# Up weight loads of the first attention wait for the landing of a minus-maxima row

## The reference

```python
xn = _layernorm(x, axis=-1)
x = x + _L0_attn_ref(xn, w_qkv, w_o) + _L0_ffn_ref(xn, gate_w, ..., down_sv)
xn = _layernorm(x, axis=-1)
x = x + _L1_attn_ref(xn, bv_q, bv_k, bv_v) + _L1_ffn_ref(xn, w1, w3, w2, ...)

def _L0_attn_ref(x, w_qkv, w_o):          # 32 heads of 16, 8 key/value heads, rope
    ...
    scores = jnp.einsum('bhsd,bhtd->bhst', xq, keys) * scale
    scores = jnp.where(causal, scores, -jnp.inf)
    probs = jax.nn.softmax(scores, axis=-1)
    out = jnp.einsum('bhst,bhtd->bhsd', probs, values)
    ...

def _L0_ffn_ref(x, gate_w, gate_su, gate_sv, up_w, up_su, up_sv, down_w, ...):
    a = _anemll_linear(x, gate_w, gate_su, gate_sv)   # w_eff = w * (su @ sv)
    b = _anemll_linear(x, up_w, up_su, up_sv)
    d = jax.nn.silu(a) * b
    return _anemll_linear(d, down_w, down_su, down_sv)
```

## Time and profile before

| | us |
|---|---|
| median of 3 runs | 719.05 |
| lowest and highest run | 716.56, 719.7 |
| the profiled execution | 718.95 |
| its span on the core | 717.2 |
| TensorE busy in the span | 687.6 (96%) |
| DVE, ScalarE, GpSimd busy | 415.0, 293.1, 237.6 |
| mean granted TensorE clock | 0.976 |

### The profile page before, as it was taken

How to read it: one execution, slowest core, us unless ns; L and a number is a source line. 1 busy time by engine, 2 the same in 40 slices (tenths; PEclk the granted TensorE clock), 3 DMA queues, 4 the chain that set the end, 5 groups by cost and what they waited for, 6 DMA issues and landing times. The chain is left out here.

```text
span 717.2 us, 10113 instructions
## 1 busy us (share of the span) xinstructions
PE 687.6 (96%) x3606; PEld 519.9 (72%) x3606; DVE 415.0 (58%) x982; ACT 293.1 (41%) x548; POOL 237.6 (33%) x241
## 2 busy tenths in 40 slices
PE   8997999999999999999999999879999999978998
PEld 7876666666666666666787788757888888856886
DVE  6634876776676676664377650297554554635611
ACT  4213255554555455455344232254334444332421
POOL 4465022332222222222234535233232322203443
PEclk9999799999999999999999999969999999997999
DMA  9328515323313232311155500020000100103211
GB/s 304 106 91 234 127 31 134 75 73 73 72 44 73 74 80 70 83 45 45 48 179 164 192 16 1 22 87 30 31 30 30 60 30 1 42 7 97 60 58 59
DMA packets 23147, 55.19 MB, mean 77 GB/s; under 512 B 3733, under 2 KB 4089, under 8 KB 22041
## 3 DMA queue, kind: packets, MB, share of 16 engines
q1 hardware_dynamic: 22840, 54.41, 26.5%
q10 hardware_dynamic: 256, 0.13, 0.1%
HBM read 42.86 MB, written 11.54 MB: 76 GB/s over the span
## 5 line engine op out<-in xcount | busy, mean ns | idle before, releaser
L956 DVE CUSTOM_DVE_ANT_0 bank<-bank,mask 128x512 f32<-128x512 f32 (+3 forms) x256 | 118.4, 523 | 64.1 <-PE bank L1010 63.9
L214 POOL TENSOR_TENSOR up_w_lo<-up_w_eff,up_w_hi 128x512 fp32r<-128x512 f32 x50 | 66.3, 1335 | 121.7 <-ACT up_w_hi L210 121.7
L52 PE MATMUL bank<-x0T_hi,up_w_hi 128*128 128x512 f32 x224 | 97.1, 434 | 4.8 <-DVE up_gated L280 2.5
L364 POOL TENSOR_TENSOR down_h_lo<-hidden,down_h_hi 128x512 fp32r<-128x512 f32 x50 | 65.8, 1316 | 106.6 <-ACT down_h_hi L359 106.5
L910 ACT ACTIVATE probs<-bank 128x512 f32<-128x512 f32 x160 | 85.3, 598 | 28.2 <-PE bank L1032 25.4
L54 PE MATMUL bank<-x0T_lo,up_w_hi 128*128 128x512 f32 x224 | 89.9, 401 | 0.0
L53 PE MATMUL bank<-x0T_hi,up_w_lo 128*128 128x512 f32 x224 | 89.5, 399 | 0.0
L52 PE MATMUL bank<-down_w_hi,down_h_hi 128*128 128x512 f32 x200 | 79.5, 398 | 1.1 <-DVE down_w_lo L349 0.7
L875 POOL TENSOR_SCALAR_AFFINE_SELECT probs<-probs 128x512 f32<-128x512 f32 x64 | 40.0, 637 | 122.1 <-ACT probs L910 122.1
L53 PE MATMUL bank<-down_w_hi,down_h_lo 128*128 128x512 f32 x200 | 78.9, 395 | 0.0
L54 PE MATMUL bank<-down_w_lo,down_h_hi 128*128 128x512 f32 x200 | 78.9, 394 | 0.0
(11 more groups left out here) (146 smaller groups left out, 1275.2 us busy)
## 6 DMA issues: line engine op xcount, KB each, us to landing
w_raw<-in_w_gate_up SPq DMA_DIRECT2D x25, 512.0 KB, 4.2
w_raw<-in_w_down SPq DMA_DIRECT2D x25, 256.0 KB, 2.7
q_stack<-q_hi SPq DMA_DIRECT2D x32, 128.0 KB, 3.5
att<-att_T SPq DMA_DIRECT2D x16, 256.0 KB, 2.1
q_hi<-rope_hi SPq DMA_DIRECT2D x8, 256.0 KB
q_lo<-rope_lo SPq DMA_DIRECT2D x8, 256.0 KB
q_stack<-q_lo SPq DMA_DIRECT2D x16, 128.0 KB, 3.7
attention_or_xn<-att SPq DMA_DIRECT2D x16, 128.0 KB
```

Of the source, the lines that this page charges most:

```text
L52: pe.matmul(out, w_hi, m_hi, start=first, stop=False, skip_group_check=True)
L214: pool.tensor_tensor(self.half(self.w_lo[:, o % 2], k), self.half(self.w_eff, k), f32(self.half(self.w_hi[:, o % 2], k)), ALU.subtract).th ...
L364: pool.tensor_tensor(self.h_lo[:, k % 2, :], self.hid[:, o, b * S:(b + 1) * S], f32(self.h_hi[:, k % 2, :]), ALU.subtract).then_inc(self.h ...
L956: dve.tensor_tensor_reduce(out=own, in0=own, in1=e.mask[:, S - w:S], scale=1.0, scalar=NEG, op0=ALU.add, op1=ALU.max, accum_out=rmax[:, i, ...
```

## The change

SyncE gets a wait ahead of each up load. `row_near(step)` looks from two steps back to three steps ahead for a burst in which a minus-maxima row is sent, and returns the semaphore of that row and the value that it has once the row has landed. SyncE waits for it and only then sends the load. By the schedule this gives: up(3), up(6), up(9), up(12) wait for the low row of group 0, 4, 8, 12 (sent one step earlier in the order of steps); up(5), up(8), up(11) for the high row of group 3, 7, 11 (also one step earlier), and up(4), up(7), up(10), up(13) for the high row of group 2, 6, 10, 14 (sent two steps later). up(2) finds none and is not held. The order of the transfers on SyncE's queue stays as it was.

```diff
+        def row_near(step):
+
+            for near in range(step - 2, step + EVERY + 1):
+                s = stages_of(burst_after(near)) if burst_after(near) is not None else {}
+                if s.get("high") is not None:
+                    return neg_row[1], 16 * (s["high"] + 1)
+                if s.get("low") is not None:
+                    return neg_row[0], 16 * (s["low"] + 1)
+
         def sync(sp):
             def store(g):
                 sp.wait_ge(att_out, g + 1)
@@ -848,6 +857,8 @@
                 if factor_before(step - 1) and factor_before(step - 1)[1] == 1:
                     o = factor_before(step - 1)[0] + 1
                     if o < CH0:
+                        if row_near(step):
+                            sp.wait_ge(*row_near(step))
                         up.sp_load(sp, o)
                     if o == 4:
                         sp.wait_ge(e.lr0_lo, 2 + len(LR0_REST))
```

## The result

| | before | after |
|---|---|---|
| median, 19 runs each, us | 716.75 | 714.12 |
| lowest to highest run | 714.28 to 721.11 | 712.85 to 718.19 |
| the profiled execution | 718.95 | 717.56 |
| its span | 717.2 | 715.8 |
| low row of group 0 to low row of group 15, in the profile | 243.74 | 241.25 |

The ratio after to before is 0.9965, with an interval of 0.9949 to 0.9982: 0.35% less time, about 2.5 us of the 716.75. The loop in the profile is shorter by 243.74 - 241.25 = 2.49 us, the same amount.

A forecast was written before the change was run, and what follows sets the result against it. TensorE was taken to bound the first attention, so only its waits could be regained. 2.69 us saved less 0.3 lost gave 2.39 off 718.95: 716.6 us, or 0.33% less, with an 8-in-10 range of 714.9 to 719.6.

The forecast's parts named there:

- the base of 718.95 us: Time of the profiled execution before the change, from which the forecast saving was subtracted; 0.1 below the median of 719.05.
- the same 2.39: Net saving forecast for the whole kernel in us: 2.69 saved on row waits, 0.3 lost to the factors.
- rival 1: All five waits at groups 4, 5, 8, 9, 12 go and the factors cost nothing: 715.6, or 715.5; chance 0.2.
- TensorE as the bound, the loss passing through one for one: First attention, 84 to 345 us: TensorE busy 259.09 of 261 us; each wait lengthens the loop by its idle time.
- 2.69 us booked on the loads at 5, 8 and 12: Low-row waits of 0.89, 0.68 and 1.12 us, blamed on up loads issued 0.32 us ahead of the row.
- Waits at 4 and 9 booked on the stack: Low-row waits of 0.40 and 0.23 us, 0.63 together, blamed on stack transfers and taken as no gain.
- The factors at 0.3 us, bounds 0 and 1.12: 864 KB of down-weight factors, issued later behind up(4), may make the low row of group 2 wait; cost taken 0.3.
- The prediction's last line: Signs of being wrong: groups 5, 8 and 12 still wait, or groups 2, 3, 6, 7, 10 or 11 begin to.
- A row's landing at 2.1 us or a little more: High row's time from issue to landing, 2.1 to 2.4 us expected, taken from the 256 KB store's 2.1 us.
- Rival 2: The loads are not the cause, or stack transfers take their place; only the 0.3 moves, about 719; chance 0.15.
- Rival 3: Loads behind high rows run into the following stack, delaying six low rows by at most 1.12 us each; 723.0; chance 0.08.
- the rule of the Trainium skill that spoke against the change: DMA engines alternate between queues packet by packet, so a row waits for a packet, not a load; saving near zero.

The follow-up runs named there:

- low rows only: Changed kernel with only up(3), up(6), up(9) and up(12) waiting, for the low rows of groups 0, 4, 8, 12; ratio to before 0.9958.
- changed again: The changed kernel unaltered, measured and profiled a second time against the kernel before; ratio 0.9969, loop 240.23 us.

## Why the prediction was right or wrong

**The time of 716.6 and its range were wrong, the difference was right.** The change was forecast at 0.33% less and measured at 0.35%. The median of 714.12 lies below the range's low end of 714.9. The step that failed is the first term of the sum, the base of 718.95 us from which everything was subtracted. I noted that it was 0.1 from the median of three runs and gave the base itself hardly any width; over 19 runs the median of before is 716.75, 2.2 us lower. From that base the same 2.39 gives 714.4. The low end of 714.9 left only 0.6 us below rival 1's lowest figure, 715.5, for all spread of the base, and the lowest of the three runs, 716.56, already spoke for a lower one: less 2.39 it is 714.2. The base also moves from one set of runs to another: beside the experiments its median was 718.0 in 29 runs and 716.25 in 14. The profiles show parts of the spread: the low row of group 0 is sent at 90.4 to 93.6 us in the twelve profiles, and what lies behind the last low row takes 379.8 to 381.3. The kernel before went from 243.74 to 242.74 for its loop from one profile to the next, because the waits at 3, 4 and 9 were in the first only. So the profiled execution held about 1 us of waits that come and go.

Another part lies ahead of the loop. From 75 to 80 us the granted TensorE clock was 0.50, the lower level of 1.2 GHz, in the first profile of before, and 1.00, the upper level of 2.4 GHz, in its repetition. The clock fell at 70 to 75 us (0.62) in the first and at 65 to 70 (0.66) in the repetition; TensorE had been busy for 2.7 of 5 us from 60 to 65 in both. In the four profiles with 0.50 from 75 to 80 (before, low rows only, changed, changed again) the low row of group 0 is sent at 92.0 to 93.6 us; in the six with 1.00 and without the wait for the high row of group 0, at 90.4 to 91.3. Before and changed kernels are among both, so this is spread and not an effect of the change. Over the changed kernel's 19 runs, the five with a mean granted clock of 0.976 or less took 715.2 to 718.2 us and the seven with 0.983 or more 712.9 to 713.7; in the 29 and 14 runs of before the two go together only weakly. The profiled execution of before had 0.976. What moves the drop was not tried.

**TensorE as the bound, the loss passing through one for one: right.** With waits gone at 5, 8 and 12, the spacings fell by 0.92, 0.68 and 1.13, to within 0.03 of the excess read before.

**2.69 us booked on the loads at 5, 8 and 12: right.** These waits stay wherever these loads do not move, go as each load moves, and shrink with half the bytes.

**Waits at 4 and 9 booked on the stack: partly right.** The 0.31 at group 9 without any load shows that the stack can do it alone; with load and row issued together the key score of group 9, again without a load, began 0.24 us late. At group 4 the row landed in 2.58 to 3.28 us with the stack alone, in the five kernels that show it, below the 3.64 of before; where the load stood there 0.8 to 1.05 us behind the row, no wait is listed three times (the key scores began 0.03 to 0.20 us late), and 0.43 and 0.23 once each. I called that load innocent; the runs neither clear it nor convict it. In all four cases of a wait at 4 or 9 (0.43, 0.25, 0.23, 0.31) that group's stack had a slow issue, but such issues also stand in profiles without a wait there, so that they decide is likely and not shown.

**The factors at 0.3 us, bounds 0 and 1.12: place and bounds right, the reason not.** The new wait stood at group 2, 0.92 us in one of the three profiles with the factors at that place and absent in the other two, where the stack had a slow issue. With the factors moved it left that group in two kernels whose stack came as usual. The mean of the three is 0.3 by luck: it was chosen because the factors would be nearly done, and they landed about 2.4 us after the row was sent. The prediction's last line also counts a wait that begins at group 2 as a sign of being wrong, a few lines behind allowing one there; the experiments put it down to the factors and not to the load behind a high row.

**A row's landing at 2.1 us or a little more: 1.71 in fact**, when nothing is near. up(4) then landed in 3.6 us, and in the changed kernel's profile no combine of DVE waited for an up load.

**The rivals.** Rival 1, all five waits gone, is what the changed kernel's profile shows, but its price of 3.32 counted 0.63 that the kernel before does not pay in its second profile, and it had the factors at nothing. Rival 2 fell with the moved loads and with half the load. Rival 3, the slower one, needed high rows to land after 3.5 us; they took 1.7, and groups 6, 7, 10 and 11 show no wait in the changed kernel's two profiles.

On the rule of the Trainium skill that spoke against the change ("DMA: Bandwidth & Descriptors", section "Queues, rings and completion order"), the measurement decides: turns between queues did not protect a row of 4 KB from one 512 KB load issued with it, 3.71 us against 1.71. That a completion lands only behind earlier writes, the same section's other statement, agrees with it, though no run here separates the two causes.

## What to carry to other kernels

A small transfer on the critical path can be late because of a large one on another queue, at a price that goes with the large one's bytes (here about 0.6 us for each 256 KB). Ask how much spare time the small one has with its regular neighbours, here 0 to 0.5 us, then move what can wait, and look at what moves with it in order on the same queue. Compare equal places of a repeating loop to read effects of tenths of a microsecond, and do not base an absolute time on one profiled execution or three runs: take the base's own spread into the range.

## What was not expected of the hardware

The issue of one transfer on SyncE's queue, 0.42 us as a rule, took 0.9 to 2.4 us now and then, at much the same places (2.42 at 156.16 in the changed kernel, 1.78 at 154.35 before). It shifts the rest of a stack behind the row or against it, and probably makes waits of up to 0.4 us come and go. Its cause was not tried.

A load issued within 0.01 us of the row delayed it by 2.0 us, with no stack near. With one issued 0.24 us behind the row, and the stack ahead of it, the key score began at most 0.13 us late.
